# A selective state-space scan: products with B on TensorE as matmuls with diagonal matrices, passes of 4 states by half the tokens, C products on GpSimd

## The reference

```python
xin, z = split(h @ in_proj_w.T)              # 1024 channels each
xin = silu(causal_conv4(xin) + conv_b)
dt, B, C = split(xin @ x_proj_w.T, [32, 48])  # B, C: 16 states per token
delta = softplus(dt @ dt_proj_w.T + dt_proj_b)
A = -exp(A_log)                               # 1024 x 16
for t in range(512):
    h = exp(delta[t][:, None] * A) * h + (delta[t] * xin[t])[:, None] * B[t]
    y[t] = (h * C[t]).sum(states)
out = ((y + xin * D) * silu(z)) @ out_proj_w.T
```

## Time and profile before

| | us |
|---|---|
| three runs: lowest, median, highest | 2384.49, 2387.05, 2387.55 |
| the profiled execution | 2386.14 |
| its span in the trace | 2384.4 |
| busy in the span: PE, DVE, ACT, POOL | 2257.4, 1982.9, 1622.3, 700.8 |
| stage `mamba_inputs` | 1690 to 1744 |
| the 64 passes of `mamba_scan` | 1744 to 1956 |
| its norm and transposes | 1956 to 1973 |

### The profile page before, as it was taken

The page is one execution under the profiler, slowest core; times in us unless marked ns, Lnnn a source line. Parts: engine busy times, 40 slices in busy tenths (PEclk is TensorE's granted clock), DMA queues, the critical chain, the costliest instruction groups (busy, mean ns, idle before and its releaser), DMA issues. The chain is left out here.

```text
span 2384.4 us, 51863 instructions
## 1 busy us (share of the span) xinstructions
PE 2257.4 (95%) x20287; PEld 1264.2 (53%) x20287; DVE 1982.9 (83%) x1910; ACT 1622.3 (68%) x2006; POOL 700.8 (29%) x494
## 2 busy tenths in 40 slices
PE   7999999999999889999999999999877779989998
PEld 3555555555555456666666666666322334444544
DVE  5888888888888789999999999997789982368995
ACT  5555566655665389999999999996564432248994
POOL 0555565555655320000000000000069960020001
PEclk8999999999999999999999999999989999999999
DMA  7354555546543595333333334333130023259994
GB/s 264 89 162 160 179 177 177 160 160 215 185 151 107 143 281 145 103 109 103 105 106 107 105 103 109 103 98 125 46 155 1 0 71 141 107 179 364 405 407 154
DMA packets 168911, 361.32 MB, mean 152 GB/s; under 512 B 13337, under 2 KB 84121, under 8 KB 165081
## 3 DMA queue, kind: packets, MB, share of 16 engines
q1 hardware_dynamic: 167266, 355.27, 46.4%
q0 software_dynamic: 1280, 4.20, 0.5%
q10 hardware_dynamic: 248, 0.15, 0.0%
HBM read 252.54 MB, written 107.04 MB: 151 GB/s over the span
## 5 line engine op out<-in xcount | busy, mean ns | idle before, releaser
L473 DVE TENSOR_REDUCE kv_mx<-kv_s 128x1024 f32 (+1 forms) x512 | 626.1, 1224 | 160.3 <-PE kv_s L509 160.3
L814 DVE TENSOR_TENSOR at_pl<-at_pf,at_ph 128x1024 f16<-128x1024 f32 x512 | 617.7, 1223 | 30.2 <-ACT at_ph L751 17.4
L765 ACT ACTIVATE at_pf<-at_st 128x1024 f32<-128x1024 f32 x512 | 520.8, 1021 | 63.0 <-PE at_st L916 62.1
L889 PE MATMUL at_acc<-at_vs,at_ph 128*128 128x130 f16 x4096 | 426.3, 220 | 2.2 <-DVE at_pl L814 2.2
L891 PE MATMUL at_acc<-at_vs,at_pl 128*128 128x65 f16 x4096 | 412.5, 192 | 0.0
L889 PEld LDWEIGHTS at_acc<-at_vs,at_ph 128*128 128x128 f16 x4096 | 367.0, 97 | 69.1 <-ACT at_av L757 5.7
L915 PE MATMUL at_st<-keep_big,at_k_cur 128*128 (+1 forms) x1024 | 389.3, 380 | 11.5 <-DMA keep_big<-q_dram 8.8
L891 PEld LDWEIGHTS at_acc<-at_vs,at_pl 128*128 128x128 f16 x4096 | 361.8, 98 | 57.7
L916 PE MATMUL at_st<-keep_big,at_k_one 128*128 (+1 forms) x1024 | 389.4, 380 | 0.0
L509 PE MATMUL kv_s<-kv_ksh,first_qh 64*128 64x512 f16 x1024 | 381.5, 376 | 2.5 <-DVE kv_mx L473 2.5
L751 ACT ACTIVATE at_ph<-at_pf 128x1024 f16<-128x1024 f32 x256 | 269.0, 1051 | 0.0
(11 more groups left out here) (362 smaller groups left out, 4972.1 us busy)
## 6 DMA issues: line engine op xcount, KB each, us to landing
keep_big<-gate_up SPq DMA_DIRECT2D x17, 2048.0 KB, 14.7
at_vs<-vd SPq DMA_DIRECT2D x64, 520.0 KB, 3.6
at_k_cur<-kd SPq DMA_DIRECT2D x126, 256.0 KB, 3.8
vd<-kv_vs SPq DMA_DIRECT2D x15, 2080.0 KB, 8.2
kv_tf<-wpack SPq DMA_DIRECT2D x21, 1024.0 KB, 6.8
keep_big<-down SPq DMA_DIRECT2D x17, 1024.0 KB, 15.4
first_cf<-ctxT SPq DMA_DIRECT2D x16, 1024.0 KB, 12.1
ex_yg<-gate_up SPq DMA_DIRECT2D x8, 2048.0 KB, 14.7
```

What stands on the lines that cost most here:

```text
L473: nc.vector.reduce_max(mx[:, bass.ds(g * (NH * TT) + 2 * n, 2)], s1[:, n % 2, :, :], AX.X).then_inc(s1_max, 1)
L765: nc.scalar.activation(pf[:, s % FULL, :, :], st[:, s % HP % NST, :, :], ACT.Exp, scale=SCORE).then_inc(pf_ready, 1)
L814: nc.vector.tensor_tensor(pl[:, s % RING, :, :], pf[:, s % FULL, :, :], ph[:, s % RING, :, :], ALU.subtract).then_inc(pl_ready, 1)
L889: nc.tensor.matmul(own_acc[t], ph[:, s % RING, e, tok], vs[:, 2 * s + e, :], start=first, stop=False, skip_group_check=True)
```

## The change

Passes take 4 states by half the tokens (`HN` = 4, `TH` = 256), still 1024 columns and still 64 passes: in a block f, four passes over the first half, then four over the second. A state's value at the end of the first half, times the decay of the next token, is a carry (`carry`, 128 x 4, made by VectorE) that is added into the first column of the second half's b.

b is made by TensorE, in PSUM. u of a block is turned by four transposes (`turn_u`), copied to SBUF by ScalarE (`ut`) and serves as weights; the moving operand is B as diagonal matrices, 128 x 128 for each state and token tile (`spreads`), made once in `mamba_inputs` as identity x B (`spread`: six by GpSimd, two by VectorE). B reaches the partitions by transposes of `xd` and two copies of ScalarE (`keep.bt`), so the DMAs of B go. A pass needs four matmuls of 256 columns for b, and in the second half two more of two columns each for the carry.

`hs` is now in SBUF and `b` in PSUM (two buffers). `hc` has four buffers. GpSimd makes the C products of all passes but pass 5 of a block, and u of the next block; VectorE makes pass 5's. TensorE runs b two passes ahead and the sums two passes behind. Two token tiles of the output projection go along; the others come in the last block.

```diff
-HN = 2
-PASSES = DS // HN
+HN = 4
+QS = DS // HN
+PASSES = 2 * QS
+TH = T // 2
...
-POOL_OUT = (1, 4)
...
+DVE_OUT = (5,)
...
+def spread(eng, keep, p):
+
+    return eng.tensor_tensor(diagonals(keep)[p].rearrange("p a n t -> p (a n) t"),
+                             keep.ident[:, :].unsqueeze(1).to_broadcast([P, 2 * HN, P]),
+                             keep.bt[:, p, :, :].rearrange("p a n -> p (a n)").unsqueeze(2)
+                             .to_broadcast([P, 2 * HN, P]), ALU.mult)
...
-            for q, dst in enumerate(scan_rows(keep, 0)):
-                sp.dma_start(dst, xd_dram[q * HN:(q + 1) * HN, :].partition_broadcast(P)).then_inc(next_in, 16)
-            sp.wait_ge(next_in, 16 * PASSES)
...
+            pool.wait_ge(bt_read, 2)
+            for q in POOL_SPREADS:
+                spread(nc.gpsimd, keep, q).then_inc(spread_done, 1)
...
+            act.wait_ge(bt_ready, 1)
+            for h in range(2):
+                nc.scalar.activation(keep.bt[:, h * QS:(h + 1) * QS, :, :].rearrange("p q a n -> p a q n"),
+                                     bt_bank[:, 2 * h:2 * h + 2, DR:DR + DS].rearrange("p a (q n) -> p a q n", n=HN),
+                                     ACT.Copy).then_inc(bt_read, 1)
             gate(DIC + 1, ACT.Silu)
...
-            delta(range(0, 4))
+            delta(range(0, 3))
+            pe.wait_ge(xd_read, 1)
+            for a in range(TT):
+                last = nc.tensor.transpose(bt_bank[:, a, :], xd[:, a * P:(a + 1) * P], keep.ident[0:64, 0:64])
+            last.then_inc(bt_ready, 1)
...
-        RB, RC, RS = 3, 3, 2
...
+        RB, RC, RS = 2, 4, 3
+        BEHIND = 2
...
+        U_AT, TURN_AT, GATE_AT, PROJECT_AT = 2, 5, 2, 4
+        LAST_AT = range(2, 2 + EARLY)
...
+                if q not in DVE_OUT:
+                    if q < QS:
+                        pool.wait_ge(carried, f * QS + q + 1)
+                    else:
+                        pool.wait_ge(scanned, i + 1)
...
+                    nc.gpsimd.tensor_tensor(hc[i % RC][:, :, :], hc[i % RC][:, :, :], cc[q], ALU.mult).then_inc(pool_hc, 1)
...
+            def turned(f):
+                act.wait_ge(up_ready, f + 1)
+                if f >= 2:
+                    act.wait_ge(b_ready, PASSES * (f - 1))
+                nc.scalar.activation(ut[:, f % 2, :, :], up[:, :, :], ACT.Copy).then_inc(ut_ready, 1)
...
+                    last = nc.scalar.activation(hs[i % RS][:, n, 1:], keep.delta[:, f, h * TH + 1:(h + 1) * TH], ACT.Exp,
                                                 scale=aneg[:, f, s:s + 1])
...
+                nc.vector.tensor_tensor_scan(hc[i % RC].rearrange("p n t -> p (n t)"),
+                                             hs[i % RS].rearrange("p n t -> p (n t)"),
+                                             b[:, i % RB, :, :].rearrange("p n t -> p (n t)"), 0.0,
                                              ALU.mult, ALU.add).then_inc(scanned, 1)
...
+                if q < QS:
+                    dve.wait_ge(first_a_ready, f + 1)
+                    dve.wait_ge(scanned, i + 1)
+                    nc.vector.tensor_tensor(carry[:, q, :], hc[i % RC][:, :, TH - 1], first_a[:, f, q * HN:(q + 1) * HN],
+                                            ALU.mult).then_inc(carried, 1)
...
+            def inputs(i):
+
+                f, q = passes[i]
+                if q == 0:
+                    pe.wait_ge(ut_ready, f + 1)
+                if i >= RB:
+                    pe.wait_ge(scanned, i - RB + 1)
+                h, first = divmod(q, QS)
+                if h:
+                    pe.wait_ge(carried, f * QS + first + 1)
+                for a in range(2):
+                    for pair in (slice(0, 2), slice(2, 4)):
+                        last = nc.tensor.matmul(b[:, i % RB, pair, a * P:(a + 1) * P], ut[:, f % 2, 2 * h + a, :],
+                                                spreads[q][:, a, pair, :], start=True, stop=(not h or a == 1),
+                                                skip_group_check=True)
+                        if h and a == 0:
+                            nc.tensor.matmul(b[:, i % RB, pair, 0:1], ident[:, :], carry[:, first, pair].unsqueeze(2),
+                                             start=False, stop=True, skip_group_check=True)
+                last.then_inc(b_ready, 1)
...
+                wait_outputs(pe, i)
+                h = q // QS
+                for n in range(HN):
+                    last = nc.tensor.matmul(yp[:, h * TH:(h + 1) * TH], ident[:, :], hc[i % RC][:, n, :],
+                                            start=False, stop=(q % QS == QS - 1 and n == HN - 1), skip_group_check=True)
+                last.then_inc(summed, 1)
...
+            turn_u(0)
+            for i in range(RB):
+                inputs(i)
             for i, (f, q) in enumerate(passes):
...
+                if q == TURN_AT and f + 1 < DIC:
+                    turn_u(f + 1)
+                if i + RB < NP:
+                    inputs(i + RB)
+                if i >= BEHIND:
+                    sums(i - BEHIND)
...
+            pe.wait_ge(scanned, NP)
+            out_proj(EARLY, range(TT))
+            for i in range(NP - BEHIND, NP):
+                sums(i)
             out_proj(DIC - 1, range(TT))
```

More of the change, by code:

```diff
@@ L1295, in mamba_scan @@
         m = Space(nc, ctx, "ms")
-        bb, cc = (scan_rows(keep, first) for first in (0, 2))
+        spreads, cc = diagonals(keep), scan_rows(keep)
         aneg, dk, u, ident, zero = keep.aneg, keep.dk, keep.u, keep.ident, keep.zero
-        RB, RC, RS = 3, 3, 2
-        b = [m.sb(f"b{i}", [P, HN, T]) for i in range(RB)]
-        hc = [m.sb(f"hc{i}", [P, HN, T]) for i in range(RC)]
+        RB, RC, RS = 2, 4, 3
+        BEHIND = 2
+        hs = [m.sb(f"hs{i}", [P, HN, TH]) for i in range(RS)]
+        ut = m.sb("ut", [P, 2, TT, P])
+        first_a, carry = m.sb("first_a", [P, DIC, DS]), m.sb("carry", [P, QS, HN])
+        hc = [m.sb(f"hc{i}", [P, HN, TH]) for i in range(RC)]
         xk = m.sb("xk", [P, 2, T])
@@ L1456, in _ @@
                         dve.wait_ge(c_in[q], 16)
[L1457 to L1458 removed]
+                    nc.vector.tensor_tensor(hc[i % RC][:, :, :], hc[i % RC][:, :, :], cc[q], ALU.mult).then_inc(dve_hc, 1)
+                if q == GATE_AT and f:
                     gate(f - 1)
                 if f == DIC - 1 and q == 1:
[L1461 to L1462 removed]
+                    for t in range(2):
+                        dve.wait_ge(early_ready, t + 1)
+                        nc.vector.tensor_tensor(keep.a[:, t, :], early[t], keep.a[:, t, :], ALU.add).then_inc(early_read, 1)
             gate(DIC - 1)
[L1464 removed]
+            dve.wait_ge(early_read, 2)
             dve.wait_ge(n_in, 16)
@@ L1487, in _, with turn_u, sums @@
         def _(pe):
+            def turn_u(f):
+                if f:
+                    pe.wait_ge(u_ready, f)
+                    pe.wait_ge(ut_ready, f)
+                for a in range(TT):
+                    last = nc.tensor.transpose(up[:, a, :], u[:, a * P:(a + 1) * P], ident[:, :])
+                last.then_inc(up_ready, 1)
+            def inputs(i):
+                f, q = passes[i]
+                if q == 0:
+                    pe.wait_ge(ut_ready, f + 1)
+                if i >= RB:
+                    pe.wait_ge(scanned, i - RB + 1)
+                h, first = divmod(q, QS)
+                if h:
[9 more added lines that the diff above has]
+                last.then_inc(b_ready, 1)
+            def sums(i):
+                f, q = passes[i]
+                if q == 0:
+                    if f:
+                        pe.wait_ge(y_ready, f)
+                    pe.wait_ge(xk_ready, f + 1)
+                    nc.tensor.matmul(yp[:, :], ident[:, :], xk[:, f % 2, :], start=True, stop=False,
+                                     skip_group_check=True)
+                wait_outputs(pe, i)
[4 more added lines that the diff above has]
+                last.then_inc(summed, 1)
             def out_proj(j, ts):
@@ L1492, in out_proj @@
                     tok = slice(t * P, (t + 1) * P)
[L1493 to L1496, removed]
+                    first = t < 2 and j < EARLY
+                    last = product(nc, early[t] if first else tiles[t], [(y[j][:, tok], w_out[j])],
+                                   start=(j == 0 or (t < 2 and j == EARLY)),
                                    stop=(j == DIC - 1 or (first and j == EARLY - 1)))
```

147 lines of the change are left out of this document (63 added, 84 removed).

## The result

The changed kernel takes 2449.03 us (median of six runs, 2447.20 to 2452.30) against 2386.36 us for the kernel before (2383.39 to 2388.83): 1.0264 times as long, 95% interval 1.0254 to 1.0275. The forecast was 2447.0 in a range of 2430 to 2474. The profiled execution took 2447.66 us with a span of 2445.9, against 2386.14 and 2384.4.

What follows compares the result with a forecast made beforehand. VectorE bounds the scan stage before the change, TensorE after it: stage before +1.0, filling +5.5 and 267.8 us of TensorE work put the last sums +63.3 later; less 2.4 in the tail, +60.9 on 2386.1 gives 2447.0 us, range 2430 to 2474.

Steps and rivals of the forecast that it cites:

- Who bounds: Scan stage: TensorE becomes the bound at 0.214 us per 256-column float32 record; 33 us a block where VectorE needs 20.9.
- Carries: Scan stage, TensorE: 128 two-column records at 0.109 us, taken from the transposes, make 14 us; ends 4 and 24.
- TensorE's total: Scan stage: sums 109.7, b 109.7, carries 14, xk 6.9, turning u 3.5 and out-projection 24.0 make 267.8 us.
- Filling: Start of the scan stage: TensorE waits while the pipe fills and runs at low clock; 5.5 us, ends 3 and 10.
- Stage before and tail: Ahead of the scan, ScalarE's copies and wait add 1.0 us (0 to +3); behind the last sums, 2.4 us less.
- The engines beside it: Scan stage: VectorE needs 20.9 us a block, GpSimd 17.7 and ScalarE 15, against TensorE's 33.
- A: Scan stage: TensorE is not the bound, 256-column records take at most 0.127 us, VectorE sets the stage; 2350 us, chance 4%.
- B: Scan stage: float32 weight loads stop hiding, a record takes 0.24 us, +27 us; 2474 us, chance 9%.
- C: Scan stage: GpSimd becomes the bound, its C products slowed by VectorE; at 5 us each +22, 2469 us, chance 2%.

## Why the prediction was right, step by step

- **Who bounds.** TensorE, by the rate of float32 records: forecast 0.214 us for 256 columns, scaled from 0.43 for 512; measured 0.216. The 1024 records of b and sums make 221.0 us, forecast 219.4. The float16 kernels confirm it from the other side: only fewer and shorter records of TensorE, in three experiments, made the stage shorter.
- **Carries.** Forecast 14 us by the transposes with a float32 load each, out of 4 to 24; measured 32 x 0.44 = 14. The reason given, a float32 load with no long stream to hide it, shows in the loads: behind a carry they start about 0.11 us apart, the step of the transposes that the prediction had taken, and 0.216 between longer records. In the records, two of two columns take 0.14 us and the pair of 256 columns behind them 0.51 instead of 0.43, so about a third of the price lies on the next matmul.
- **TensorE's total.** With xk 6.9, turning 3.5 and out-projection 24.0 as forecast, 221.0 + 14.1 + 34.4 = 269.5 us, forecast 267.8.
- **Filling.** What is left of 275.5 is 6.0, forecast 5.5 (3 to 10). It comes from the forecast's two sources, in other shares. The waits are 1.8 us, where the forecast counted 0.7 for ScalarE's copy and 0.7 for each of three scans, 2.8. The low clock cost more than the 2.7 that this left for it and the turning: at a mean of 0.72 in the first 12 us, the first 24 records of b alone take 8.22 us and at 0.216 would take 5.3. That the total came out within 0.5 us is in part luck.
- **Stage before and tail.** +0.5 for a forecast +1.0: ScalarE's Abs begin at 1725.36 instead of 1724.79, and its chain still ends last. GpSimd's six spreads took 1.9 us each and not 2.35 and were done by 1737.25, under ScalarE as forecast. The tail is -2.4 for -2.4.
- **The engines beside it.** VectorE 169.35 / 8 = 21.2 us a block (forecast 20.9; a carry is 0.25 in the mean, not 0.2). GpSimd's C product 2.362 (2.342). ScalarE's exponential of 255 columns was mis-sized: 0.496 us instead of 0.42, 19 us over 256 of them, hidden under 83.9 us of waiting.
- **The rivals.** A (TensorE not the bound) fell with the record's 0.216. Its mechanism is sound all the same: VectorE's work is free while the records are float32 (four C products of a block on VectorE) and sets the stage once they are not (b and sums in float16). B (loads not hidden, 0.24 a record) fell by the same 0.216. C (GpSimd the bound) fell with its 131 us of idle time and with the kernel that took 57 us of work from it for no gain.

The change is +62.6 us between the two profiled executions, for a forecast +60.9: 1.7 low, of which the records' rate is 1.6. My expectation of float16 b was too good by 13 us, for a reason that the prediction had used itself: a pipe whose bound is made shorter shows its next limit before it shows the whole gain.

## What to carry to other kernels

Moving work to an engine because it idles in part pays only if its new total, at its own rate for that type, stays under the engine that is relieved: here some 128 us of float32 records (b, carries, turning) went to the engine that already had some 140, to save 37 on one that had 206. Read a matmul's rate from the starts of records without gaps, by type: a group's mean (379 ns) says nothing about 216. And when a wait names a producer, give it one more buffer before believing that buffers are short: if the wait only changes its name and the time stays, as here, the buffers were not the limit.

## What the runs showed that I had not expected

**VectorE and GpSimd took turns.** Where the spreads of both met, the changed kernel's trace has, in order of time:

```profile
1732.49 4.76 POOL L1083 TENSOR_TENSOR keep_big<-keep_ident,mamba_bt 128x1024 f32<-128x1024 f32 x2
```

```profile
1734.28 4.05 DVE L1083 TENSOR_TENSOR keep_big<-keep_ident,mamba_bt 128x1024 f32<-128x1024 f32 x2
```

VectorE's first runs its usual 1.215 us, 1734.28 to 1735.50. GpSimd's last starts at 1734.3 and ends at 1737.25: 1735.4 and its usual 1.9. VectorE's second starts at 1735.4 and ends at 1738.33: 1737.1 and its usual 1.22. Within some 0.1 us each of the two long ones is the other engine's remainder and then its own full time. The Trainium skill says so (SBUF — State Buffer, SBUF: two separate sides): VectorE with two SBUF inputs and a GpSimd operation that reads SBUF lock each other out for a whole instruction. The trace agrees here. It did not show in the scan: the products with C have two SBUF inputs on both engines, but the longest on VectorE took 1.226 us and on GpSimd 2.368 with 32 on each, since in that kernel they stood in different halves of a block. With b and sums in float16 they touch: GpSimd's product runs from 1850.52 for 2.36 us, VectorE's starts at 1852.65, and it takes 1.31 us instead of 1.225. That fits, but no run was made to test it. The prediction had up to 4 us for such a meeting; it cost nothing, by a small margin: ahead of the scan VectorE's last instruction ends at 1743.61 and ScalarE's at 1743.70.

**The clock was lower with b and sums in float16.** Busy for all of 250 us, or 47.95 of 50 with b alone in float16, it had a granted clock of 1.00. With all records of b and sums in float16 it was busy 34.63 us of 50, at a mean of 0.86, between the levels of 1.2 and 2.4 GHz. VectorE was busy 48.19 of the same 50, so this was not what held the stage there. Gaps alone do not tell the clock: the kernel before had TensorE busy for 16.45 us of 26 at a clock of 1.00. What made the difference stays open.
